# Linear attention in split precision: high and low halves side by side in one operand

## The reference

```
x2 = layer_norm(x, ln1_g, ln1_b)
q, k, v = x2 @ wq + bq, x2 @ wk + bk, x2 @ wv + bv        # 1250 x 16 heads x 64
qp, kp = phi(q), phi(k)      # phi(x) = [cos(p), sin(p)] / sqrt(128), p = x @ proj / 8, proj 64 x 128
kv   = einsum('blhm,blhd->bhmd', kp, v)                   # per head 256 x 64, the key sums
attn = einsum('blhm,bhmd->blhd', qp, kv)
```

## Time and profile before

| | |
|---|---|
| median of 3 runs | 1334.69 us (1333.11 to 1338.66) |
| profiled execution | 1334.61 us, its span 1332.8 us |
| TensorE busy | 1247.7 us, 94% of the span |
| VectorE, ScalarE, GpSimd busy | 57%, 47%, 26% |
| mean granted TensorE clock | 0.971 |
| matmuls | 7017 |

### The profile page before, as it was taken

One profiled execution on the slowest core, in us unless ns is written; L12 is line 12 of the kernel. 1 busy time (PEld: TensorE's weight loads), 2 busy tenths in 40 slices (PEclk: granted clock), 3 DMA queues, 4 the chain that ended last, 5 costly groups with the idle time before them and its releaser, 6 DMA issues. The chain is left out here.

```text
span 1332.8 us, 19542 instructions
## 1 busy us (share of the span) xinstructions
PE 1247.7 (94%) x7017; PEld 1088.1 (82%) x7017; DVE 766.2 (57%) x1212; ACT 631.6 (47%) x917; POOL 340.5 (26%) x296
## 2 busy tenths in 40 slices
PE   6989889999999999999957999799999999899997
PEld 4556689999999999999946787699997887788874
DVE  7979625455655556565553376577774321556546
ACT  8175534555555555555554533332233442455544
POOL 1400003241423232332220201056662433021000
PEclk9999999999999999999976999899999799999999
DMA  8011310111020202020214645432335232620112
GB/s 207 10 29 25 78 36 1 33 35 54 12 66 0 66 0 66 0 66 0 67 45 150 216 151 172 137 107 81 92 91 192 74 93 62 211 72 14 50 32 93
DMA packets 72193, 99.41 MB, mean 75 GB/s; under 512 B 27241, under 2 KB 52165, under 8 KB 71631
## 3 DMA queue, kind: packets, MB, share of 16 engines
q1 hardware_dynamic: 68684, 86.11, 22.5%
q0 software_dynamic: 3456, 12.58, 3.1%
HBM read 77.04 MB, written 21.63 MB: 74 GB/s over the span
## 5 line engine op out<-in xcount | busy, mean ns | idle before, releaser
L1140 POOL TENSOR_TENSOR cos_sin_lo<-cos_sin,cos_sin_hi 125x1024 fp32r<-125x1024 f32 (+1 forms) x40 | 95.8, 2396 | 351.2 <-ACT cos_sin_hi L1214 351.2
L1201 ACT ACTIVATE cos_sin<-part_turn 125x512 f32<-125x512 f32 (+1 forms) x80 | 50.1, 627 | 152.7 <-DVE part_turn L1329 152.7
L468 PE MATMUL p_cnt<-hot_s,hot_d 125*125 125x418 bf16 x540 | 113.8, 361 | 1.8 <-DVE hot_d L401 1.8
L705 PE MATMUL p_h<-x 128*125 128x512 f32 x400 | 109.3, 400 | 0.0
L399 DVE TENSOR_SCALAR hot_s<-iota_h,ends 125x1250 bf16<-125x1250 f16 x180 | 98.2, 546 | 14.6 <-PE p_cnt L468 12.5
L468 PEld LDWEIGHTS p_cnt<-hot_s,hot_d 125*125 125x125 bf16 x540 | 63.3, 140 | 51.6 <-DVE hot_d L401 40.6
L1414 PE MATMUL p_w<-x,mix_hi_v 128*128 128x416 f32 (+1 forms) x384 | 105.2, 355 | 0.0
L1414 PE MATMUL p_w<-x,mix_hi_k 128*128 128x416 f32 (+1 forms) x384 | 104.2, 352 | 0.0
L1414 PE MATMUL p_w<-x,mix_hi_q 128*128 128x416 f32 (+1 forms) x384 | 104.1, 352 | 0.0
L966 PE MATMUL rows_in_psum<-h_hi,a_lo 125*125 125x342 f32 x300 | 96.8, 323 | 3.0 <-DVE a_lo L910 3.0
L1327 DVE TENSOR_SCALAR whole_turns<-p_p 125x512 f32<-125x512 f32 (+1 forms) x80 | 54.4, 680 | 77.0 <-PE p_p L1465 74.4
(11 more groups left out here) (302 smaller groups left out, 3169.8 us busy)
## 6 DMA issues: line engine op xcount, KB each, us to landing
x_in<-in_x_dram SPq DMA_DIRECT2D x30, 448.0 KB
attn_dram<-attn_t SPq DMA_DIRECT2D x8, 625.0 KB, 3.9
at_in<-attn_dram SPq DMA_DIRECT2D x10, 500.0 KB, 4.6
x_rows<-in_x_dram SPq DMA_DIRECT2D x10, 448.0 KB
x_in<-gnn_dram SPq DMA_DIRECT2D x10, 448.0 KB
out_dram<-rows SPq DMA_DIRECT2D x10, 448.0 KB
mix_in_v<-in_L_mix_wv_dram SPq DMA_DIRECT2D x8, 512.0 KB, 6.0
mix_in_k<-in_L_mix_wk_dram SPq DMA_DIRECT2D x8, 512.0 KB, 4.7
```

The source lines that it names most:

```text
L468: last = pe.matmul(p_cnt[0:T, t % 2, n, 0:w], hot_d[:, j, 0:T], hot_s[:, j, a:a + w], start=False, stop=False)
L705: last = pe.matmul(p_h[0:T, i % 2, n, :], left[i % 2][:, k, :], right[:, k, cols], start=(k == 0 and m == 0), stop=(k == K8 - 1 and m == 2))
L1140: pool.tensor_tensor(full(cs_lo, k), full(cs, k), f32(full(cs_hi, k)), ALU.subtract).then_inc(s_cslo[0], 1)
L1201: act.activation(step_view(cs, k, 1), rows(part, k), ACT.Sin, scale=TWO_PI)
```

## The change

Values and key sums: v_hi and v_lo become one tile v_both, for each head 64 columns high and 64 low side by side. As the stationary operand it gives both parts of one head's key sum in one matmul, 256 columns wide, on the two partition halves of the result. The key sums of one head take four matmuls of 256 columns for a block of 250 rows, both heads eight, where six of 512 columns were. `copy_kv` copies them, `transpose_kv` transposes them, then the two halves are added: ScalarE takes one into kv_sum, VectorE adds the other (`add_kv`), ScalarE writes the high and VectorE the low parts into kv_both. Attention uses kv_both as its stationary operand: 8 matmuls of 250 columns for 12, with high and low contributions of each head on the two partition halves. ScalarE keeps one half of each head in attn_t (`keep_attention`, now with semaphore s_atc), VectorE adds the other (`add_attention`) and only then sets s_atk.

Queries: q_both holds for each head the high part on its own 64 partitions and the low part on the other 64. The stationary operand proj_both holds `proj` on both halves. 4 matmuls of 250 columns for 6. `keep_run` for queries becomes two operations of 64 partitions on ScalarE and on VectorE.

The attention sums move into the second bank of the key sums (p_kv_at), so `accumulate_kv` of the next pair waits for all of s_atk. `copy_kv` moves ahead of `phases(j, 6)` on VectorE, and `value_run` is cut one block of three matmuls earlier.

The diff, shortened:

```diff
-        q_hi = sb("q_hi", [128, N], F32R)
-        q_lo = sb("q_lo", [128, N], F32R)
+
+        q_both = sb("q_both", [128, 2, N], F32R)
+        proj_both = sb("proj_both", [128, 2, KMAP], F32R)
         v_t = sb("v_t", [128, N])
-        v_hi = sb("v_hi", [T, NT, 128], F32R)
-        v_lo = sb("v_lo", [T, NT, 128], F32R)
+
...
-        kv_hi = sb("kv_hi", [128, 4, 128], F32R)
-        kv_lo = sb("kv_lo", [128, 4, 128], F32R)
+        kv_sum = sb("kv_sum", [128, 4, DH])
+
+        kv_both = sb("kv_both", [128, 4, 2, DH], F32R)
         attn_t = core.attn_t
         p_w = ps("p_w", [128, 3, 512])
         p_p = ps("p_p", [128, 2, 512])
-        p_kv = ps("p_kv", [128, 512])
-        p_at = ps("p_at", [128, 512])
+        p_kv = ps("p_kv_at", [128, 2, 512])
+        p_at = p_kv[:, 1]
...
+            pool.wait_ge(s_prep, 3)
+            for n, half in enumerate((proj_lo, proj_hi)):
+                pool.tensor_tensor(proj_both[:, n], f32(half[:, 0]), f32(half[:, 1]), ALU.add).then_inc(s_prep, 1)
...
-                out = (v_t, k_hi, q_hi)[which]
-                act.activation(out[:, a:a + w], p_w[:, n, 0:w], ACT.Identity, bias=bias[which][:, bass.ds(j, 1)]
-                               ).then_inc(s_vt if which == VALUE else s_kqhi, 1)
+                if which == QUERY:
+                    for h in range(2):
+                        head = slice(h * DH, (h + 1) * DH)
+                        last = act.activation(q_both[head, h, a:a + w], p_w[head, n, 0:w], ACT.Identity, bias=bias[which][head, bass.ds(j, 1)])
+                    last.then_inc(s_kqhi, 1)
+                else:
+                    out = (v_t, k_hi)[which]
+                    act.activation(out[:, a:a + w], p_w[:, n, 0:w], ACT.Identity, bias=bias[which][:, bass.ds(j, 1)]
+                                   ).then_inc(s_vt if which == VALUE else s_kqhi, 1)
...
-                act.activation(v_hi[:, first:first + count, :], p_tr[0:T, 0:count, :], ACT.Copy).then_inc(s_trhi, 1)
+                act.activation(v_both[:, first:first + count, :, 0], p_tr[0:T, 0:count, :].rearrange("p i (h d) -> p i h d", h=2), ACT.Copy).then_inc(s_trhi, 1)
...
+                act.activation(kv_sum[:], p_tr[:, :, DH:2 * DH], ACT.Copy, scale=1.0 / KMAP).then_inc(s_kvs, 1)
+                act.wait_ge(s_kvs, 2 * j + 2)
                 for h in range(2):
-                    last = act.activation(kv_hi[:, 2 * h:2 * h + 2, h * DH:(h + 1) * DH],
-                                          p_tr[:, 2 * h:2 * h + 2, h * DH:(h + 1) * DH], ACT.Copy, scale=1.0 / KMAP)
+                    last = act.activation(kv_both[:, 2 * h:2 * h + 2, h], kv_sum[:, 2 * h:2 * h + 2], ACT.Copy)
                 last.then_inc(s_trhi, 1)
...
-                act.activation(attn_t[:, c * CHUNK:(c + 1) * CHUNK], p_at[:, 0:CHUNK], ACT.Copy).then_inc(s_atk, 1)
+                for h in range(2):
+                    head = slice(h * DH, (h + 1) * DH)
+                    last = act.activation(attn_t[head, c * CHUNK:(c + 1) * CHUNK], p_at[head, h * CHUNK:(h + 1) * CHUNK], ACT.Copy)
+                last.then_inc(s_atc, 1)
...
-                hi, lo, s = (k_hi, k_lo, s_klo) if which == KEY else (q_hi, q_lo, s_qlo)
-                dve.scalar_tensor_tensor(lo[:, a:a + w], p_w[:, n, 0:w], bias[which][:, bass.ds(j, 1)], f32(hi[:, a:a + w]),
-                                         ALU.add, ALU.subtract).then_inc(s, 1)
+                if which == QUERY:
+                    for h in range(2):
+                        head, other = slice(h * DH, (h + 1) * DH), slice((1 - h) * DH, (2 - h) * DH)
+                        last = dve.scalar_tensor_tensor(q_both[other, h, a:a + w], p_w[head, n, 0:w], bias[which][head, bass.ds(j, 1)],
+                                                        f32(q_both[head, h, a:a + w]), ALU.add, ALU.subtract)
+                    last.then_inc(s_qlo, 1)
+                else:
+                    dve.scalar_tensor_tensor(k_lo[:, a:a + w], p_w[:, n, 0:w], bias[which][:, bass.ds(j, 1)], f32(k_hi[:, a:a + w]),
+                                             ALU.add, ALU.subtract).then_inc(s_klo, 1)
...
-                dve.tensor_tensor(v_lo[:, first:first + count, :], p_tr[0:T, 0:count, :],
-                                  f32(v_hi[:, first:first + count, :]), ALU.subtract).then_inc(s_trlo, 1)
+                dve.tensor_tensor(v_both[:, first:first + count, :, 1], p_tr[0:T, 0:count, :].rearrange("p i (h d) -> p i h d", h=2),
+                                  f32(v_both[:, first:first + count, :, 0]), ALU.subtract).then_inc(s_trlo, 1)
+
+            def add_kv(j):
+                dve.wait_ge(s_kvs, 2 * j + 1)
+                dve.scalar_tensor_tensor(kv_sum[:], p_tr[:, :, 0:DH], 1.0 / KMAP, kv_sum[:], ALU.mult, ALU.add).then_inc(s_kvs, 1)
...
-                    block_h = (slice(None), slice(2 * h, 2 * h + 2), slice(h * DH, (h + 1) * DH))
-                    last = dve.scalar_tensor_tensor(kv_lo[block_h], p_tr[block_h], 1.0 / KMAP, f32(kv_hi[block_h]),
-                                                    ALU.mult, ALU.subtract)
+                    last = dve.tensor_tensor(kv_both[:, 2 * h:2 * h + 2, 1 - h], kv_sum[:, 2 * h:2 * h + 2],
+                                             f32(kv_both[:, 2 * h:2 * h + 2, h]), ALU.subtract)
                 last.then_inc(s_trlo, 1)
+
+            def add_attention(j, c):
+
+                dve.wait_ge(s_atc, STEPS * j + c + 1)
+                for h in range(2):
+                    head, other = slice(h * DH, (h + 1) * DH), slice((1 - h) * DH, (2 - h) * DH)
+                    here = attn_t[head, c * CHUNK:(c + 1) * CHUNK]
+                    last = dve.tensor_tensor(here, here, p_at[other, h * CHUNK:(h + 1) * CHUNK], ALU.add)
+                last.then_inc(s_atk, 1)
 
...
-                dve.tensor_copy(kv_t[:], p_kv[:].rearrange("p (b m) -> p b m", b=4)).then_inc(s_kvt, 1)
+                dve.tensor_copy(kv_t[:].rearrange("p (h c) m -> p h (c m)", h=2), p_kv[:, :, 0:2 * KMAP]).then_inc(s_kvt, 1)
...
                 phases(j, 5)
+                copy_kv(j)
                 phases(j, 6)
-                copy_kv(j)
                 keep_lo(j, 5)
+                add_kv(j)
                 keep_kv(j)
                 phases(j, 7)
+                add_attention(j, 0)
                 if more:
                     keep_run(KEY, j + 1, 0)
...
                 keep_lo(j, 9)
+                add_attention(j, 3)
                 if more:
                     phases(j + 1, 0)
                     keep_run(KEY, j + 1, 2)
+                    add_attention(j, 4)
                     phases(j + 1, 1)
                 else:
...
-                    for m, (left, right) in enumerate(((proj_lo, q_hi), (proj_hi, q_lo), (proj_hi, q_hi))):
-                        last = pe.matmul(p_p[:, k % 2, h * CHUNK:(h + 1) * CHUNK], left[:, h, :], right[:, c * CHUNK:(c + 1) * CHUNK],
-                                         start=(m == 0), stop=(m == 2))
+                    for m in range(2):
+                        last = pe.matmul(p_p[:, k % 2, h * CHUNK:(h + 1) * CHUNK], proj_both[:, m], q_both[:, h, c * CHUNK:(c + 1) * CHUNK],
+                                         start=(m == 0), stop=(m == 1))
...
+                    pe.wait_ge(s_atk, STEPS * j)
...
-                    for m, (left, right) in enumerate(((v_lo, hi), (v_hi, lo), (v_hi, hi))):
-                        last = pe.matmul(p_kv[:], left[:, 2 * k + i, :], right[:, i].rearrange("p h c m -> p (h c m)"),
-                                         start=(k == 0 and i == 0 and m == 0), stop=(k == STEPS - 1 and i == 1 and m == 2))
+                    for m, right in enumerate((lo, hi)):
+                        for h in range(2):
+                            last = pe.matmul(p_kv[:, h, 0:2 * KMAP], v_both[:, 2 * k + i, h].rearrange("p a d -> p (a d)"),
+                                             right[:, i, h].rearrange("p c m -> p (c m)"),
+                                             start=(k == 0 and i == 0 and m == 0), stop=(k == STEPS - 1 and i == 1 and m == 1))
...
-                    cols = slice(b * CHUNK, (b + 1) * CHUNK)
-                    for m, (left, right) in enumerate(((kv_lo, cs_hi), (kv_hi, cs_lo), (kv_hi, cs_hi))):
-                        last = pe.matmul(p_at[:, 0:CHUNK], left[:, b, :], right[:, k % 2, cols],
-                                         start=(b == 0 and m == 0), stop=(b == 3 and m == 2))
+                    h = b // 2
+                    for m, right in enumerate((cs_lo, cs_hi)):
+                        last = pe.matmul(p_at[:, h * CHUNK:(h + 1) * CHUNK], kv_both[:, b].rearrange("p a d -> p (a d)"),
+                                         right[:, k % 2, b * CHUNK:(b + 1) * CHUNK],
+                                         start=(b % 2 == 0 and m == 0), stop=(b % 2 == 1 and m == 1))
...
-                    value_run(j + 1, 2, 0, half)
+                    value_run(j + 1, 2, 0, half - 1)
                 transpose_kv(j)
                 if more:
```

(5 more changed lines are left out.)

10 lines of the change are left out of this document (7 added, 3 removed).

## The result

| | before | after |
|---|---|---|
| median | 1334.17 us in the runs beside it | 1370.46 us (4 runs, 1368.81 to 1373.84) |
| ratio | | 1.0269, 95% interval 1.0242 to 1.0296 |
| profiled execution, its span | 1334.61, 1332.8 us | 1368.81, 1367.0 us |
| mean granted TensorE clock | 0.971 | 0.959 |

The direction was as forecast. The size was not: +36 us where the forecast was +12.7, and outside its range of 1321 to 1362.

What follows compares the result with a forecast made beforehand. TensorE bounds the loop before; after, the VectorE-ScalarE hand-over at 66.3 us a round. First pair -3.4, six rounds +11.4, last pair +4.7: +12.7 on 1334.61 gives 1347.3 us, range 1321 to 1362.

Steps and rivals of the forecast that it cites:

- the ring: VectorE-ScalarE hand-over in the attention loop, 61.65 us a round before; would set the pace: 1341 to 1357 us, chance 0.53.
- The waits: TensorE's waits in a loop round, about 8.2 us: key sums (some 4), first attention step (2.1), fourth (1.1).
- The ring's sum: VectorE-ScalarE hand-over chain with all additions and savings: 66.3 us a round, 1.9 above before.
- half operations: Operations on half the partitions; for queries on ScalarE and VectorE, 3 x 1.06 = +3.2 us a round.
- S8: Start of VectorE's first operation of step 8's phases; S0 to S9 name the ten steps' starts likewise.
- Change of partitions: Half operations alternating between partitions 0 and 64: 0 to 1.2 us a round, middle taken, +0.6.
- Collision with GpSimd: VectorE's low halves of the key sums beside GpSimd's low part of step 6: end about 0.95 us later.
- the old one: VectorE's collision with GpSimd at step 3, 2.15 us before the change; shrinks, -1.05 us a round.
- Attention adds: VectorE's adds of attention-sum halves for steps 8 and 9, ahead of the next pair's phases: +1.3 us a round.
- The first pair: Attention stage up to the second pair's first key sum: that key sum starts at 260.9, -3.4 us.
- The clock: Rival: TensorE's clock falls behind the new wait before the first attention step, +1.7 us a round, 1360 us, chance 0.10.
- The last pair: Last pair of heads, a chain without products to overlap: +4.7 us, bounds 0 and +9.

Runs made afterwards that it cites:

- experiment 4: Changed kernel, with GpSimd starting its low part of step 6 only after the key sums' low halves: 1361.68 us, ratio 1.0194.
- experiment 5: Changed kernel without VectorE's adds of the second halves of the attention sums (left out, sums unfinished): 1351.64 us, ratio 1.0132.
- 8: Changed kernel plus experiment 4's wait, with VectorE's low parts of steps 1 and 9 and step 8's attention add behind the following phases: 1349.24 us, ratio 1.0114.
- experiment 3: Changed kernel, VectorE's half operations all starting at partition 0 (query halves on 128 partitions, ScalarE too; adds into scratch; results wrong): 1357.56 us, ratio 1.0154.
- experiment 9: Changed kernel plus 14 unused 250-column matmuls on TensorE in its wait ahead of the first attention step: 1365.45 us, ratio 1.0211.

## Why the prediction was right in direction and wrong in size

- **TensorE would lose the bound to the ring**: right. The waits are the forecast ones, and experiments 4, 5 and 8 shorten the round without taking work from TensorE. The waits forecast at 8.2 us a round (the list of them adds up to 7.2) are 7.4.
- **The ring's sum**, 66.3 us: measured 67.63 at full clock. The places without half operations came out within 0.2 us: last key sum to first attention step 8.65 (forecast 0.95 for its matmuls + 5.8 + 1.75 = 8.5), from there to S8 9.34 (9.96 - 0.7 = 9.3), S8 to S9 5.63 (5.7). Three of those with them did not: S9 to S0 7.28 in place of 6.8, S0 to S1 6.30 in place of 5.8, S1 to S2 8.01 in place of 7.4. From S2 to S4 it is 15.81 in place of 15.6.
- **"Change of partitions ... I take the middle, +0.6"**: failed. It is 1.6 us (experiment 3), above the upper end of 1.2. I had counted the lost overlap of neighbours (0.08) on one engine. The rows show 0.23 per pair on VectorE and 0.14 on ScalarE. The Trainium skill, VectorE: DVE Perf Modes, section Two Vector instructions with no wait between them, lets an instruction that starts in another quadrant (32 partitions) than the last one used start only when the earlier ones are done. The trace agrees: 1.35 us is two whole durations of 0.65 in a row and 0.05, 1.12 is two that overlap. The middle between a rule and its absence was no estimate.
- **Collision with GpSimd, 0.95**: right (experiment 4: 0.95). What is left of the old one: 0.6 at each of two steps, 1.2 where 1.1 was forecast.
- **Attention adds, 1.3**: 2.0 (experiment 5), of which 0.46 is the change of partitions again; 0.2 too little.
- **The first pair, -3.4**: failed, 0.0. S2 was to follow at 201.5 and starts at 203.38, behind the low part of 3.13 us, a collision of the kind that was counted in the loop and not here. From S2 to the second pair's first key sum it takes 60.9 us in place of 59.4: the clock fell behind the wait for kv_both there too. In experiment 9, where it did not, this stretch is 59.3.
- **The clock**, put at 0.10 as a rival and left out of the sum: it happened, in every other round. The wait it hangs on was forecast at 2.1 us, above the 1.8 that I had named as the point from which it decides; by the prediction's own numbers its chance should have been well above 0.10. It costs 1.6 us each time (1.7 forecast) and fell three times, twice within the six rounds; without it the stretch from the first to the last transposes is 5.5 us shorter (experiment 9), the one larger collision below included.
- **The last pair, +4.7**: failed, +10.8, above its upper end of 9. I had counted the adds as two short operations in each step. There is nothing to overlap here, so TensorE waits for each add behind the phases queued ahead of it, and the shifted order made a new collision. Before, TensorE waited for attn_t as well (4.16, 3.20 and 0.56 us, for ScalarE's keep). TensorE and VectorE in the last pair, with the row of before last:

```profile
718.53 0.55 PE L1531 MATMUL p_kv_at<-cos_sin_lo,kv_both 128*128 128x250 f32 x1 [3.16 <-DVE attn_t L1353]
724.59 0.55 PE L1531 MATMUL p_kv_at<-cos_sin_lo,kv_both 128*128 128x250 f32 x1 [3.16 <-DVE attn_t L1353]
732.15 0.55 PE L1531 MATMUL p_kv_at<-cos_sin_lo,kv_both 128*128 128x250 f32 x1 [4.67 <-DVE attn_t L1353]
736.52 0.55 PE L1531 MATMUL p_kv_at<-cos_sin_lo,kv_both 128*128 128x250 f32 x1 [2.33 <-DVE attn_t L1353]
```

```profile
725.62 3.35 DVE L1373 TENSOR_TENSOR x<-mix_in_q,x 128x1024 fp32r<-128x1024 f32 x1
728.88 0.67 DVE L1360 TENSOR_SCALAR whole_turns<-p_p 128x500 f32<-128x500 f32 x1
...
695.20 1.22 DVE L1340 TENSOR_TENSOR x<-mix_in_q,x 128x1024 fp32r<-128x1024 f32 x1
```

The low part of a weight (725.62) took 1.22 before (695.20) and now stands beside GpSimd's 725.47 + 2.42: step 9 starts 2.1 us later.

The profiled executions differ by 34.2 us, 21.5 more than forecast. The first pair is 3.4 of it, and all behind the stage gives 0.3 back. The rounds are 12.3 (23.7 - 11.4): the clock 3.2, the partitions 6 x 1.0, the rest of the ring 6 x 0.38, and one larger collision in the first of them, 0.8 (third phase operation of step 2, 2.05 us in place of 1.32). The last pair is 6.1. Of its 8.9 us behind the transposes 5.2 are the adds (experiment 5); that the collision makes up 2.1 of the rest is read from the rows and was not tried. So the direction came from the right mechanism, but no single term carries the miss: the change of partitions, the clock, the first pair and the last pair each came out above what was put in the sum.

## What to carry to other kernels

Halving matmuls by putting two operands side by side pays on TensorE and is billed to the engines that fill and add the halves; price both chains for one round before choosing, and take only the parts that the slower chain hardly sees (here the key sums, 0.7% faster than before, with GpSimd's wait). On a chain of two elementwise engines, an operation on half of the partitions costs as much as a whole one, and more if neighbours change halves. Of each new wait ask two things more: does it make TensorE idle as long as the waits behind which its clock fell (1.8 us and more here), and does it set a two-input operation of VectorE beside GpSimd; both can be mended with one wait or some idle matmuls.
